# Every third cast of the shared stage from ScalarE to GpSimd in a routed gated MLP

## The reference

```python
def mlp(x, gate_w, up_w, down_w):                 # 128 -> 512 -> 128
    g = einsum('bsh,hi->bsi', x, gate_w)
    u = einsum('bsh,hi->bsi', x, up_w)
    return einsum('bsi,ih->bsh', gelu(g) * u, down_w)

w, sel = top_k(softmax(cond_8), 2)                # per sample; w normalised to sum 1
out = sum over the 8 skills e of dense_w[:, e] * mlp(x, skill e)
x = x + out + mlp(x, shared weights)
```

## Time and profile before

| what | value |
|---|---|
| median of 3 runs | 214.25 us (214.05 to 214.81) |
| profiled execution: its own time | 215.19 us |
| its span, first to last instruction | 213.3 us |
| granted TensorE clock over the span | 1.0 |
| busy share: TensorE, VectorE, ScalarE, GpSimd | 98%, 58%, 63%, 51% |
| casts of hidden rows on ScalarE (L290) | 92, mean 609 ns |
| subtractions on GpSimd (L258) | 92, mean 1158 ns |

### The profile page before, as it was taken

One profiled execution on the slowest core, in us unless ns is written; L12 is line 12 of the kernel. 1 busy time (PEld: TensorE's weight loads), 2 busy tenths in 40 slices (PEclk: granted clock), 3 DMA queues, 4 the chain that ended last, 5 costly groups with the idle time before them and its releaser, 6 DMA issues.

```text
span 213.3 us, 6740 instructions
## 1 busy us (share of the span) xinstructions
PE 208.4 (98%) x2736; PEld 167.7 (79%) x2736; DVE 123.8 (58%) x223; ACT 134.2 (63%) x217; POOL 107.7 (51%) x109
## 2 busy tenths in 40 slices
PE   7989999999999999999999999999999999999995
PEld 2444555555444458899999999999999999999995
DVE  4187996688999998644435435435435435435341
ACT  6243675788988978665665655655655655655650
POOL 3000335444574666656565565565565565565562
PEclk9999999999999999999999999999999999999999
DMA  6999500000000000000010010010010010010011
GB/s 210 426 433 433 218 5 0 3 0 0 2 3 0 0 0 5 0 3 5 3 52 0 3 52 3 3 52 0 3 54 3 3 49 3 5 52 3 3 52 49
DMA packets 2813, 11.70 MB, mean 55 GB/s; under 512 B 352, under 2 KB 608, under 8 KB 2400
## 3 DMA queue, kind: packets, MB, share of 16 engines
q1 hardware_dynamic: 2640, 11.01, 12.7%
q10 hardware_dynamic: 144, 0.26, 0.5%
HBM read 9.18 MB, written 2.10 MB: 53 GB/s over the span
## 4 chain that ended last, share of the span: by engine, by line
PE 95%; DVE 3%; issue 1%; POOL 0%; DVEq 0%; POOLq 0%
PE g_ps L594 7%; PE u_ps L594 7%; PE o_ps L611 7%; PE o_ps L612 7%; PE u_ps L593 7%; PE g_ps L593 7%; PE o_ps L613 7%; PE u_ps L595 7%; PE g_ps L595 7%; PE n_ps L528 4%; PE u_ps L561 3%; PE u_ps L563 3%; PE u_ps L562 3%; PE o_ps L574 3%; PE o_ps L576 3%; PE o_ps L575 3%
## 5 line engine op out<-in xcount | busy, mean ns | idle before, releaser
L258 POOL TENSOR_TENSOR h<-h 128x512 f16<-128x512 f32 x92 | 106.0, 1158 | 100.7 <-ACT h L290 49.8
L412 DVE SCALAR_TENSOR_TENSOR h<-gel,sk_factor,u_ps 128x512 f32<-128x512 f32 x64 | 47.8, 747 | 68.1 <-ACT gel L285 68.1
L285 ACT ACTIVATE gel<-g_ps,sk_gate 128x512 f32<-128x512 f32 x64 | 44.0, 687 | 50.0 <-PE g_ps L595 50.0
L290 ACT CAST h<-h 128x512 f16<-128x512 f32 x92 | 56.0, 609 | 1.7 <-DVE h L412 1.7
L595 PE MATMUL g_ps<-x,wsk 128*128 128x128 f16 x256 | 46.2, 219 | 0.0
L595 PE MATMUL u_ps<-x,wsk 128*128 128x128 f16 x256 | 46.2, 219 | 0.0
L594 PE MATMUL u_ps<-x,wsk 128*128 128x128 f16 x256 | 46.1, 219 | 0.0
L594 PE MATMUL g_ps<-x,wsk 128*128 128x128 f16 x256 | 46.1, 219 | 0.0
L593 PE MATMUL g_ps<-x,wsk 128*128 128x128 f16 x256 | 46.1, 219 | 0.0
L593 PE MATMUL u_ps<-x,wsk 128*128 128x128 f16 x256 | 46.1, 219 | 0.0
L613 PE MATMUL o_ps<-h,wsk 128*128 128x128 f16 x256 | 45.9, 219 | 0.0
(11 more groups left out here) (97 smaller groups left out, 305.3 us busy)
## 6 DMA issues: line engine op xcount, KB each, us to landing
wsk<-skills SPq DMA_DIRECT2D x3, 2048.0 KB, 15.4
outT<-xT SPq DMA_DIRECT2D x7, 256.0 KB, 2.0
xT<-xT SPq DMA_DIRECT2D x2, 768.0 KB, 5.8
wsh<-shared SPq DMA_DIRECT2D x3, 256.0 KB, 3.6
xT<-xT ACTq DMA_DIRECT2D x1, 256.0 KB, 3.2
xT<-xT SPq DMA_DIRECT2D x1, 256.0 KB, 4.3
outT<-xT SPq DMA_DIRECT2D x1, 192.0 KB, 1.9
outT<-xT SPq DMA_DIRECT2D x1, 64.0 KB, 1.5
```

What stands on the lines that cost most here:

```text
L258: nc.gpsimd.tensor_tensor(hidden_lo(t), hidden_full(t), hidden_hi(t), ALU.subtract).then_inc(lo_ok, 1)
L285: nc.scalar.activation(gel[:, t % NG, :], g_ps[t % 2][:, :], ACT.Gelu_apprx_tanh, scale=scale).then_inc(gelu_ok, 1)
L290: nc.scalar.copy(hidden_hi(t), hidden_full(t)).then_inc(hi_ok, 1)
L412: nc.vector.scalar_tensor_tensor(out=h32[:, t % N32, :], in0=gel[:, t % NG, :], scalar=factor, in1=u_ps[t % 2][:, :], op0=ALU.mult, op1=AL ...
```

## The change

For the rows t = 12, 15, 18, 21, 24, 27 and 30 the cast is taken off ScalarE. GpSimd waits for the f32 row (`h_ok`) instead of for ScalarE's cast, copies it into the high half with conversion to f16, waits for its own copy (a new semaphore `hi_pool`), and then goes on with the waits for the splits and the subtraction as before. For the other rows it waits for the number of casts that ScalarE has made so far. The waits for a split (`x_lo_ok`, `sk_lo_ok`) stand behind the copy. Nothing else is changed.

```diff
+        hi_pool = sem("hi_pool")
...
+        def cast_on_pool(t):
+            return 10 <= t < SH and t % 3 == 0
+
+        def casts_by(t):
+            return sum(not cast_on_pool(i) for i in range(C, t + 1))
...
             for t in range(C, STEPS):
-                pool.wait_ge(hi_ok, t - C + 1)
+                if cast_on_pool(t):
+                    pool.wait_ge(h_ok, t + 1)
+                    nc.gpsimd.tensor_copy(hidden_hi(t), hidden_full(t)).then_inc(hi_pool, 1)
+                    pool.wait_ge(hi_pool, sum(cast_on_pool(i) for i in range(t + 1)))
+                else:
+                    pool.wait_ge(hi_ok, casts_by(t))
 
                 if t in X_AT:
                     pool.wait_ge(x_lo_ok, X_NTH[X_AT[t]])
...
-                if t > C:
+                if t > C and not cast_on_pool(t - 1):
                     cast(t - 1)
```

## The result

The changed kernel takes 215.38 us (median of 22 runs) against 214.50 of the kernel before (22 runs). The ratio is 1.0036, 95% interval 1.0025 to 1.0048: **0.77 us slower**, between 0.53 and 1.03. The forecast was 0.76. One of the 22 runs of the changed kernel took 270.48 us at a granted clock of 0.758 and is left out of the ratio, which is formed over the other runs and not from the two medians (these lie 0.88 apart).

The account below looks back on a forecast made before the run. TensorE, busy 208.4 of 213.3 us, was taken as the bound. VectorE, held by GpSimd's copies and subtractions, would start row 23 0.76 us later: median 214.25 + 0.76 = 215.0 us, range 213.9 to 216.1.

Parts of the forecast that it names:

- The bound and the ceiling: TensorE bounds the kernel; its one wait from 33 us on, 0.48 us in step 25, is all the change can win.
- The copy and the wait behind it: On GpSimd, per moved row: a copy of 0.53 us and a wait for itself of 0.24, together 0.77 to 1.40.
- Row 18: the split first, the copy behind it: VectorE's skill split from 56.25 ends at 57.87 as before; GpSimd's copy 18 follows, 57.87 to 58.40.
- The next split gets in between subtractions 18 and 19: VectorE's next skill split, issued at 59.47, passes at the boundary of 59.80 and ends at 60.88 instead of 61.37.
- Which table is held: Of VectorE's small instructions before row 23, L386 meets copy 21, ending at 63.70; L390 is held by subtraction 21 to 65.10.
- The sum: Over rows 18 to 23: row 23 begins at 65.27 instead of 64.51, +0.76 us; TensorE's wait goes from 0.48 to 1.24.
- What was costed at nothing: The copies of rows 12, 15, 24, 27 and 30 cost nothing; ScalarE's seven dropped casts are not on TensorE's chain.
- The rival of the slow copy: GpSimd's copies 18 and 21 take 1.16 us like the subtraction: +2.02 us, 216.3 us; chance 0.18.
- Tables slipping through: VectorE's L390 comes ahead of subtraction 21, row 23 begins 0.24 us earlier: 214.0 us, or 214.3; chance 0.25.

## Why the prediction was right, and where its steps were not

- **The bound and the ceiling.** Right. TensorE waits once, and the change could move the time only through that wait.
- **The copy and the wait behind it.** The free copy took 0.61, near the 0.53 taken from the memset and far from the subtraction's 1.16 (the 769 ns that the prediction quotes for a loop of 512 elements was not met either). The wait of GpSimd for itself cost 0.09 (62.57 to 62.66), not the 0.24 of the earlier trace rows. The sum, 0.70, was predicted as 0.77.
- **Row 18: the split first, the copy behind it.** Right: split to 56.82, copy to 57.28, that is 57.86 and 58.32 in before's time, against 57.87 and 58.40.
- **The next split gets in between subtractions 18 and 19.** Wrong. It was issued at 58.51, and subtraction 19 had begun at 58.48. It came 0.03 too late and was held to the end of the pair: it ended at 61.76 in before's time, not at 60.88. The boundary had been put at 59.80 and came at 59.52, mostly because copy 18 ended 0.46 behind the split instead of 0.53 and the wait cost 0.09 instead of 0.24; the split had been put at 59.47 and came at 59.55.
- **Which table is held.** Wrong by one. The prediction had L386 held by the copy and L390 by the subtraction; held were L384 and L387. The text named the loss of the earlier boundary as the other possibility, but had L390 caught there too; with a wait of 0.09 subtraction 21 began in time for L387.
- **The sum.** +0.76 predicted, +0.79 in the trace, 0.77 in the runs. That they lie so close is luck, since two steps were off by about as much in opposite directions. Subtraction 21 ended at 64.85 in before's time instead of 65.07, 0.22 earlier, mainly because each of the two waits of GpSimd for its own copy cost 0.09 instead of 0.24. Against it, the held table had two tables behind it (L403, L406) instead of one: row 23 began 0.43 behind its end (63.84 to 64.27) instead of 0.17. That the split ended 0.88 later than predicted makes no difference between the two sums: the tables came 0.88 later too, and the first of them was held to the end of copy 21, which came at 63.61 in before's time, near the 63.67 of the prediction. The mechanism was right and has its place; the agreement within 0.03 is not owed to the single steps.
- **What was costed at nothing.** Right: five copies (ratio 1.0000 without rows 18 and 21), ScalarE's casts (wait 1.28 with them kept).
- **The rival of the slow copy**, "each 0.1 us counts twice". Wrong as a rule. A copy 0.56 longer cost 0.35 at row 21 and 0.09 at row 18. The length also decides which instruction meets which boundary, and that can give part of it back.
- **Tables slipping through.** They did not in any of the kernels in which row 18 or 21 was copied on GpSimd and the tables stood behind row 22.

## What to carry to other kernels

Work moved to an engine with time to spare can still cost: not by its length alone, but by whom it excludes while it runs. Before moving work to GpSimd, look in VectorE's timeline for small instructions with durations that are too long, and see whether they end with an instruction of GpSimd; where the chain of TensorE runs over them, move them to a place where GpSimd waits. Here the kernel came out 0.2% faster with that one move, and 0.4% faster with the move and the change, where the change alone had added 0.4%.

## What the hardware showed that I had not expected

**A start 0.02 earlier is not enough.** A VectorE instruction that the trace starts up to 0.02 before the next GpSimd instruction is still held for all of it: L384 of the kernel before at 62.61 against subtraction 21, which begins at 62.62, and L400 of the change at 62.65 against 62.66. One that starts 0.14 before is through in its usual time (L399 at 62.52, for 0.22), and one that waits 0.58 gets in between two that follow each other. What decides between 0.02 and 0.14 was not tested. And GpSimd is held in its turn: 1.60 for a copy behind a split, 0.61 alone. In the trace such a copy looks slow; it only waits.

**The start of the program has no fixed length.** The first f32 matmuls of before and of after:

```profile
4.75 2.05 PE L542 MATMUL g_ps<-xT,wsh 128*128 128x512 f32 x2
```

```profile
4.93 1.10 PE L555 MATMUL g_ps<-xT,wsh 128*128 128x512 f32 x2
```

The same two passes took 2.05 us in one execution and 1.10 in the other, right behind the warm-up matmuls, and nothing later gives the difference back. In the ten profiled executions they take between 1.10 and 2.05, and the matmul of step 9 starts between 31.20 and 32.55: at 31.20 to 31.48 in the four with 1.10, at 31.41 to 31.98 in the three with 1.23 to 1.66, and at 32.36 to 32.55 in the three with 2.05, without any order by kernel. That is about as wide as the spread of the runs. The granted clock of the page is 1.0 in both executions shown; what makes the difference was not tested and stays open.
